# Attention constants built in the third group from three-term products, with their inputs prepared on VectorE, ScalarE and GpSimd

## What is computed

```python
up_gate = jnp.einsum('bsd,hd->bsh', x, W1)
up_lin = jnp.einsum('bsd,hd->bsh', x, W3)
hidden = fwht(jax.nn.silu(up_gate) * up_lin)          # both blocks' ffn
out = jnp.einsum('bsh,dh->bsd', hidden, W2)
...
# block 1, s: attention over a second layernorm, then gamma and beta
q, k, v = x_norm @ qkv[:, :KEY], x_norm @ qkv[:, KEY:2*KEY], x_norm @ qkv[:, 2*KEY:]
scores = where(causal, q @ k.T * scale, -inf)
out = softmax(scores) @ v @ o_proj + residual
```

## Time and profile before

| | us |
|---|---|
| median of 3 runs (356.45 to 356.65) | 356.49 |
| profiled execution, time | 356.77 |
| profiled execution, span | 355.0 |
| TensorE busy | 349.0 |
| VectorE busy | 252.7 |
| ScalarE busy | 167.2 |
| GpSimd busy | 106.1 |

### The profile page before, as it was taken

The page is one execution under the profiler, slowest core; times in us unless marked ns, Lnnn a source line. Parts: engine busy times, 40 slices in busy tenths (PEclk is TensorE's granted clock), DMA queues, the critical chain, the costliest instruction groups (busy, mean ns, idle before and its releaser), DMA issues.

```text
span 355.0 us, 4951 instructions
## 1 busy us (share of the span) xinstructions
PE 349.0 (98%) x1769; PEld 296.2 (83%) x1769; DVE 252.7 (71%) x498; ACT 167.2 (47%) x324; POOL 106.1 (30%) x122
## 2 busy tenths in 40 slices
PE   7999999999999999999999999999999999999996
PEld 4877888888888888888978878888888888888896
DVE  5679964995499666966488876788557886466645
ACT  2865442447244713454465643654346544464510
POOL 2164510366126943663025030150300703004000
PEclk9999999999999999999999999999999999999999
DMA  7989759206160303130341401616014251054001
GB/s 243 250 173 231 151 103 129 83 20 143 37 145 15 120 0 118 34 118 0 118 127 45 129 2 60 185 38 194 4 58 142 69 164 45 3 189 133 3 2 59
DMA packets 69648, 34.44 MB, mean 97 GB/s; under 512 B 40692, under 2 KB 69624, under 8 KB 69624
## 3 DMA queue, kind: packets, MB, share of 16 engines
q1 hardware_dynamic: 69480, 34.06, 38.0%
q10 hardware_dynamic: 144, 0.07, 0.1%
HBM read 21.99 MB, written 12.12 MB: 96 GB/s over the span
## 4 chain that ended last, share of the span: by engine, by line
PE 89%; SPq 4%; DMA 2%; ACT 2%; DVE 2%; issue 1%; ACTq 0%
PE GU L356 19%; PE GU L358 18%; PE GU L357 18%; PE O L356 8%; PE O L357 8%; PE O L358 8%; DMA stage<-in_L_ffn_W 2%; SPq L241 1%; SPq L232 1%; PE O L424 1%; PE T L357 1%; PE T L358 1%; PE T L356 1%; SPq L302 1%; PE O L507 1%; PE O L506 1%
## 5 line engine op out<-in xcount | busy, mean ns | idle before, releaser
L718 ACT ACTIVATE hf<-GU 128x512 f32<-128x512 f32 x64 | 38.2, 599 | 79.9 <-DVE hid L835 63.7
L991 DVE TENSOR_TENSOR hf<-hf,GU 128x512 f32<-128x512 f32 x64 | 43.5, 679 | 28.5 <-PE GU L358 22.6
L356 PE MATMUL GU<-XT,W1T 128*128 128x512 f32 x128 | 50.6, 396 | 0.1
L835 DVE TENSOR_TENSOR hid<-hf,hid 128x512 fp32r<-128x512 f32 x64 | 50.5, 791 | 0.3
L358 PE MATMUL GU<-XT,W1T 128*128 128x512 f32 x128 | 49.9, 390 | 0.0
L357 PE MATMUL GU<-XT,W1T 128*128 128x512 f32 x128 | 49.9, 390 | 0.0
L356 PE MATMUL GU<-XT,W3T 128*128 128x512 f32 x128 | 49.8, 389 | 0.0
L358 PE MATMUL GU<-XT,W3T 128*128 128x512 f32 x128 | 49.8, 389 | 0.0
L357 PE MATMUL GU<-XT,W3T 128*128 128x512 f32 x128 | 49.8, 389 | 0.0
L356 PE MATMUL O<-hid,W2hi 128*128 128x512 f32 x112 | 43.9, 392 | 0.0
L357 PE MATMUL O<-hid,W2hi 128*128 128x512 f32 x112 | 43.7, 390 | 0.0
(11 more groups left out here) (201 smaller groups left out, 717.7 us busy)
## 6 DMA issues: line engine op xcount, KB each, us to landing
swap_rows<-GX SPq DMA_DIRECT2D x7, 512.0 KB, 3.3
sT<-swap_rows SPq DMA_DIRECT2D x28, 128.0 KB, 2.7
swap_gate<-GX SPq DMA_DIRECT2D x7, 512.0 KB, 2.9
sT<-swap_gate SPq DMA_DIRECT2D x28, 128.0 KB, 2.7
stage<-in_L_ffn_W SPq DMA_DIRECT2D x12, 256.0 KB, 4.5
swap_p<-PX SPq DMA_DIRECT2D x4, 640.0 KB, 3.2
PL<-swap_p SPq DMA_DIRECT2D x16, 160.0 KB, 3.2
stage<-in_L_ffn_W SPq DMA_DIRECT2D x32, 64.0 KB, 2.6
```

The source lines that it names most:

```text
L356: pe.matmul(o, lhs(0), rhs(0), start=start, stop=False)
L718: act.activation(hf[:, c % 2, :], GU[:, c % 2, 0, :], ACT.Silu).then_inc(silu_done, 1)
L835: dve.tensor_tensor(dst, src, hi_part.bitcast(F32), ALU.subtract).then_inc(done, 1)
L991: dve.tensor_tensor(hf[:, c % 2, :], hf[:, c % 2, :], GU[:, c % 2, 1, :], ALU.mult).then_inc(mul_done, 1)
```

## The change

- `small_av` leaves the first group. It now stands in the third group (n = 2), behind up chunk 0, and makes each of its eight products by `mm3` from high parts avH and residues avL: 24 fp32r matmuls in the place of eight of fp32.
- VectorE's `turn_wqkv` moves from the first group to the second (n = 1), behind chunk 5.
- ScalarE gets four copies for avH behind chunk 6 of the second group; GpSimd gets four subtractions for avL (`av_residues`) in the second group, ahead of its second pair of weight residues.
- The high parts and residues of AR and VR are made behind chunk 2 of the third group, on ScalarE and VectorE. The Hadamard matmul of that group moves from behind chunk 1 to behind chunk 2, with the wait for sm_lo at 3 ahead of it; ScalarE's copy of its result moves from behind chunk 2 to behind chunk 3.
- In memory, wqkvT and wo take the room that AR and VR fill later, and avH and avL take room of block 1's W1 and W3 tiles whose columns are written later in the third group.

```diff
--- before.py
+++ after.py
@@ -68,6 +68,9 @@
 
         X = sb("X", [P, NB * TILES, D])
         MR = sb("MR", [P, 2, KC, D], F32R)
+        with ExitStack() as early:
+            wqkvT = sb("wqkvT", [P, 3, KC, D], F32, early)
+            wo = sb("wo", [P, KC, D], F32, early)
         AR = sb("AR", [P, 2, KC, D], F32R)
         VR = sb("VR", [P, 2, KC, D], F32R)
         ident = sb("ident", [P, P])
@@ -111,12 +114,13 @@
         with ExitStack() as early:
             win = sb("win", [P, MC, D], F32, early)
             woutT = sb("woutT", [P, MC, D], F32, early)
-            wo = sb("wo", [P, KC, D], F32, early)
-            wqkvT = sb("wqkvT", [P, 3, KC, D], F32, early)
             ssm = sb("ssm", [P, 5, MC, DS], F32, early)
             kprod = sb("kprod", [P, 2, MC, DS], F32, early)
             kvec = sb("kvec", [P, MC], F32, early)
             gbrow = sb("gbrow", [2 * KC, P], F32, early)
+        with ExitStack() as early:
+            avH = sb("avH", [P, 2 * TILES, KC, D], F32R, early)
+            avL = sb("avL", [P, 2 * TILES, KC, D], F32R, early)
         W1T = (W1T0, sb("W1T1", [P, 2, KC, H], F32R))
         W3T = (W3T0, sb("W3T1", [P, 2, KC, H], F32R))
         U, U2, W2hi, W2lo = [], [], [], []
@@ -185,6 +189,7 @@
         w_turned, wx_hi, wx_lo, natx_hi, natx_ready = sem("w_turned"), sem("wx_hi"), sem("wx_lo"), sem("natx_hi"), sem("natx_ready")
         kv_loaded = sem("kv_loaded")
         wout_loaded, wqkv_loaded, wo_loaded = sem("wout_loaded"), sem("wqkv_loaded"), sem("wo_loaded")
+        av_hi, av_lo = sem("av_hi"), sem("av_lo")
         wout_turned, wqkv_turned, win_scaled = sem("wout_turned"), sem("wqkv_turned"), sem("win_scaled")
         xnext_loaded = sem("xnext_loaded")
         w2_loaded, w2_turned = sem("w2_loaded"), sem("w2_turned")
@@ -427,18 +432,18 @@
 
             def small_av():
 
-                pe.wait_ge(wqkv_turned, 3)
-                pe.wait_ge(wo_loaded, 16)
-                for i in range(KC):
-                    for c in range(KC):
-                        last = pe.matmul(T[:, 0, i * D:(i + 1) * D], wqkvT[:, 0, c, i * P:(i + 1) * P], wqkvT[:, 1, c, :],
-                                         start=(c == 0), stop=(c == KC - 1))
-                last.then_inc(sm_mm, 1)
-                for i in range(KC):
-                    for c in range(KC):
-                        last = pe.matmul(T[:, 1, i * D:(i + 1) * D], wqkvT[:, 2, c, i * P:(i + 1) * P], wo[:, c, :],
-                                         start=(c == 0), stop=(c == KC - 1))
-                last.then_inc(sm_mm, 1)
+                pe.wait_ge(av_lo, 4)
+                pe.wait_ge(u_ready, PAIRS + 1)
+
+                def part(w):
+
+                    return lambda a, c: (avH, avL)[a][:, 2 * w + 1, c, :]
+
+                for q, (left, right) in enumerate(((part(0), part(1)), (part(2), part(3)))):
+                    for i in range(KC):
+                        for c in range(KC):
+                            last = mm3(T[:, q, i * D:(i + 1) * D], lambda a: left(a, c)[:, i * P:(i + 1) * P], lambda a: right(a, c), c == 0, c == KC - 1)
+                    last.then_inc(sm_mm, 1)
 
             def first_x_transposes():
 
@@ -548,10 +553,8 @@
                 up_chunk(0, 0, 6, True)
                 small_m()
                 up_chunk(0, 0, 7, True)
-                small_av()
                 pe.wait_ge(sm_lo, 1)
                 recurrent_mix(0)
-                pe.wait_ge(sm_lo, 3)
 
             def block0_group(n):
                 if n == 1:
@@ -560,7 +563,11 @@
                     down_chunk(0, n - 1, i)
                 for c in range(HC):
                     up_chunk(0, n, c, False)
-                    if c == 1 and n > 1:
+                    if c == 0 and n == 2:
+                        small_av()
+                    if c == (2 if n == 2 else 1) and n > 1:
+                        if n == 2:
+                            pe.wait_ge(sm_lo, 3)
                         next_hadamard(PAIRS + 2 * n - 3)
                 if n < 3:
                     next_hadamard(PAIRS + 2 * n - 2)
@@ -759,7 +766,6 @@
                 w2_hi(0)
                 chunk(0, 7, True)
                 hid_hi_chunk(0, 7)
-                small_hi([(flat[1], T[:, 0, :]), (flat[2], T[:, 1, :])], 2, sm_mm, 2, sm_hi)
 
             def block0_group(n):
                 act.wait_ge(hid_ready, 8 * n)
@@ -769,7 +775,13 @@
                 act.wait_ge(ssq_ready, 4 * n)
                 for c in range(HC):
                     chunk(n, c, False)
-                    if c == 2 and n > 1:
+                    if c == 6 and n == 1:
+                        for w in range(3):
+                            hi(avH[:, 2 * w + 1, :, :], wqkvT[:, w, :, :], wqkv_turned, w + 1, av_hi)
+                        hi(avH[:, 7, :, :], wo[:, :, :], wo_loaded, 16, av_hi)
+                    if c == 2 and n == 2:
+                        small_hi([(R[:, 0, :, :].rearrange("p k d -> p (k d)"), T[:, q, :]) for q, R in enumerate((AR, VR))], 2, sm_mm, 2, sm_hi)
+                    if c == (3 if n == 2 else 2) and n > 1:
                         pair_u(1, PAIRS + 2 * n - 3, 2 * n - 3)
                     if c == 3 and n < 3:
                         turned_hi(PAIRS + 2 * n - 2)
@@ -1021,6 +1033,11 @@
                         turn_w(PAIRS + 2 * n - 1)
                     if c == 7:
                         turn_w2(2 * n - 1)
+                if c == 5 and n == 1:
+                    turn_wqkv()
+                if c == 2 and n == 2:
+                    small_lo(1)
+                    small_lo(2)
                 if c == 0 and not last:
                     stats(n + 1, ((n + 1) % NB) * TILES)
                 if c == (4 if n < NB else 3) and not last:
@@ -1091,7 +1108,6 @@
                 chunk(0, 5)
                 x_turn(1)
                 chunk(0, 6)
-                turn_wqkv()
                 w2_sums(0)
                 small_lo(0)
                 w2_lo(0, 0)
@@ -1099,8 +1115,6 @@
                 w2_lo(0, 1)
                 dve.wait_ge(xrest_loaded, 16)
                 dve.wait_ge(small_loaded, 16 * N_SMALL)
-                small_lo(1)
-                small_lo(2)
                 hid_lo_chunk(0, HC - 1)
 
             def block0_group(n):
@@ -1253,6 +1267,12 @@
                 pool.wait_ge(natx_hi, j + 1)
                 pool.tensor_tensor(w2nat[:, 1, :, :], U2[1][:, 2 * j:2 * j + 2, :], w2nat[:, 0, :, :].bitcast(F32), ALU.subtract).then_inc(natx_ready, 1)
 
+            def av_residues():
+
+                for w, src in enumerate((wqkvT[:, 0, :, :], wqkvT[:, 1, :, :], wqkvT[:, 2, :, :], wo[:, :, :])):
+                    pool.wait_ge(av_hi, w + 1)
+                    pool.tensor_tensor(avL[:, 2 * w + 1, :, :], src, avH[:, 2 * w + 1, :, :].bitcast(F32), ALU.subtract).then_inc(av_lo, 1)
+
             def rms_of(n):
                 pool.wait_ge(ssq_ready, 4 * n + 4)
                 pool.tensor_tensor(rtmp[:, :], ssq[:, :], rms_eps[:, :], ALU.add).then_inc(rms_step, 1)
@@ -1295,6 +1315,8 @@
                 if n > 1:
                     pair_butterfly(1, 2 * n - 3, PAIRS + 2 * n - 2)
                     quad_butterfly(1, n - 2, (17, 23)[n - 2])
+                if n == 1:
+                    av_residues()
                 if n < 3:
                     pair_lo(PAIRS + 2 * n - 1)
                 else:
```

## The result

The changed kernel takes **365.12 us** (median of 5 runs, 364.19 to 365.99) against 356.49 (356.45 to 356.65); the ratio is 1.0233 with a 95% interval of 1.0216 to 1.025. The forecast was 361.3 and its range ended at 364.2. The profiled execution is the slowest of the five, 365.99 us with a span of 364.2.

A forecast was written before the change was run, and what follows sets the result against it. The prediction took the sum of TensorE's work to bound the kernel: -3.45 + 2.88 + 5.31 + 0.07 = +4.8 us, carried to the median of 356.49 as 361.3 us. The 8-in-10 range was 360.6 to 364.2.

The forecast's parts named there:

- fp32 products gone: First group (head): removing eight fp32 constant products from TensorE saves 3.45 us, if nothing else is late there.
- second group: Second group: later Wqkv transposes delay chunk 6's multiply, so the mix starts at 80.88 instead of 80.81; 0.07 us lost.
- three-term products: Third group, behind up chunk 0: 24 fp32r matmuls of 0.12 us add 2.88 us on TensorE.
- the wait: Third group, behind chunk 2: TensorE waits for VectorE's VR residue before the Hadamard matmul; costs 5.3 us, bounds 4.6 to 6.5.
- slow clock and restart: Rival, behind the third group's wait: idleness drops TensorE to half clock, 1.8 us more, total 363.1 us; chance 0.34.
- the trace alone, which has no gap after its start: Sign against the slow clock: judged by the earlier profile only, the sum would not take its 1.8 us.
- the warm-up: Kernel start: four matmuls 0.90 us apart instead of 0.43, read as half clock from 1.45 to 5.0; basis for 1.8 us.
- The head's cover: First group: last hid residue expected near 45.9, wanted by the down-projection at 46.9; 1 us margin, cost nothing.
- GpSimd's rival: Second group: GpSimd's added residues delay the third group's up-projection by 1.0 us more, total 362.3 us; chance 0.10.
- The forecast chain: Second group: GpSimd residues, weight pair, scaling, then xT's residue ending at 93.3 to 95.6, wanted at 94.55; middle just met.
- the clock's own bounds: Slow-clock case behind the third group's wait: 0.9 to 3.6 us extra, total 362.2 to 364.9 us.

The follow-up runs named there:

- the second profile of the changed kernel: The changed kernel run again unaltered: median 364.38 us over four runs, the profiled execution 364.21 us.
- the run of the first group's order: Changed kernel with products ahead of third-group up chunk 0, first-group MR residue before the W2 sum, chunk 7 before W2 parts: 356.15 us, repeated 356.84.
- the product form alone: Like the run of the first group's order, but products as eight fp32 matmuls in the same third-group place, without their input copies and residues: 357.19 us.
- residues first: Changed kernel with the AR and VR residues ahead of the four gate products behind chunk 2 of the third group: 361.55 us.

## Why the prediction was wrong

By its own terms, in the second profile of the changed kernel (364.21) against the profile before (356.77), difference 7.4 us, from the starts of TensorE's stages: `small_m` 34.74 against 35.16, the first down-projection 44.49 against 47.67, the third group's up-projection 91.44 against 94.55, the Hadamard matmul at its end 124.24 against 116.76.

| term | predicted | measured |
|---|---|---|
| fp32 products gone | -3.45 | -2.76, of it +0.69 by the late residue of MR |
| second group | +0.07 | +0.07 (46.95 against 46.88 us) |
| three-term products | +2.88 | +2.88 |
| the wait | +5.31 | +5.20 |
| slow clock and restart | 0 in the forecast, +1.8 as a rival | +2.5 |
| first group ahead of `small_m`, loads | 0 | -0.42 here, +1.5 in the first profile |

**The wait** was right to 0.1 us in place, cause and size. Its reasoning, VectorE's list behind the chunk's last matmul, is also what the experiments confirm from the other side: with the products one step earlier the wait is met, and with the gate products behind the residues it halves.

**The clock is the step that failed.** The sum put it at nothing; it measured 2.3 to 2.5 us. The prediction decided it by "the trace alone, which has no gap after its start", gave it 0.34, and named the Trainium skill's rule in "TensorE: Matmul & The Clock Gate", section "HAM oscillation — how this bites in real kernels". The trace of the changed kernel agrees with that rule: 0.50 of the clock for 4.9 us behind a gap of 5.05. The run with 20 extra matmuls shows that the idleness is the cause. The absence of gaps in the trace before was no evidence against it; the start, at half speed after idleness, was the only row that bore on the question, and it spoke for it. The price was near: 1.8 us from the warm-up against 2.3 in spacings (12 spacings from 107.71 to 112.86 took 5.15 us, at 0.227 they would be 2.7, and 0.1 is the restart itself).

**The head's cover was checked at the wrong consumer.** The prediction looked at the last residue of hid, which the down-projection wants, and cost nothing. That residue was in time: it ended at 46.50, and TensorE did not wait for it. The nearer consumer was the mix itself, which lost the 3.45 us of products that stood between it and the residue of MR. The trace before had the row for it:

```profile
41.09 0.68 DVE L835 TENSOR_TENSOR MR<-O,MR 128x512 fp32r<-128x512 f32 x1
```

It ended at 41.77, 0.43 us behind the 41.34 at which the prediction let the mix begin. The 1.81 us of the removed transposes would have covered that, but VectorE gained next to none of them: its sum behind them stood still for GpSimd's butterfly and ended at 40.91 instead of 41.17. The rule for that is in the Trainium skill, "SBUF — State Buffer", section "SBUF: two separate sides": between a VectorE instruction with two SBUF inputs and a GpSimd instruction that reads SBUF, the one that starts first has the shared ports for its whole length and the other waits fully. The trace agrees: the sum, started after the butterfly, took 3.40 us instead of 1.60 and ended 1.09 us after it. The residue of MR has one of its inputs in PSUM and took 0.69 us beside the butterfly, in the run of the first group's order.

**GpSimd's rival did not happen.** In the second profile the residue of xT ended at 90.7 and the up-projection started at 91.44 without a wait: a margin of 0.7 us. The forecast chain let the residue end 1.3 us early to 1.0 us late and left no margin in its middle, so it came in the earlier half.

**What the forecast lacked in spread.** The range ended 0.9 us under the median. It took only part of the clock's own bounds, which end at 364.9 and would not have held 365.12 either, and nothing for the residue of MR or for the loads of the first group. The forecast with 2.3 us of clock and 0.7 of MR would be 364.3, which the second set of runs has (364.38); the first set lies 0.7 above that, and its profile shows late loads. The prediction had read that all of TensorE's waits before lie in the first eight microseconds. One does not: the wait of O for a load, 0.4 us, ends at 25.66 us, and there the loads came later still in the first profile of the changed kernel (0.4 and 1.1 us of waiting, up to 27.13).

## What to carry to other kernels

When TensorE is the bound, look at every new wait for what the producing engine has in its list between the event that releases it and the value wanted; the sum of that list is the price, and it could be read here from the rows before to 0.1 us. If the gap is of several microseconds, add the slow clock behind it, or move the wait, or fill the gap. When work is taken away from an engine, look for what becomes the next wait of the nearest consumer, and whether the freed time only turns into standing before a shared port.

## What the runs showed of the hardware that I had not expected

A gap of 2.65 us brought TensorE's clock down in one profile, and one of 2.78 us did not in another; of the twelve executions of these two kernels ten lost it (mean clock 0.994 or 0.995), of the nine of the changed kernel all did. Twenty useless matmuls in the wait are worth 2.3 to 3.0 us. The granted clock column reads 1.00 over the warm-up, whose spacing is that of the half clock, but 0.50 behind a gap, so at the very start the spacing has to be read instead. Two profiles (the product form alone, residues first) show the same late event, the gate's scatter taking 1.8 and 1.9 us instead of 0.4 right behind a queue of loads, with 1.4 and 1.9 us of waiting on TensorE some 13 us after its issue; TensorE's earlier arrival brings the two closer together, but whether that makes it more frequent stays open.
